# Probabilities times values as one fp32 product per head pair in a fused cross-attention and mixture-of-experts kernel

## The reference, cut to what matters

```python
# x: 8 batches x 512 queries x 512;  ctx: 8 x 64 keys x 128;  16 heads of 32
q  = layernorm(x) @ Wq.T                    # 512 x 512
k, v = split(ctx @ Wkv_expand.T)            # each 64 x 512 per batch
scores = (q_h @ k_h.T) / sqrt(32)           # per head h, 512 x 64
scores = where(causal, scores, min)         # query i sees keys 0..i
attn = softmax(scores)
o  = attn @ v_h                             # the product that is changed
x  = x + concat(o) @ Wout.T
h  = layernorm(x)
logits = h @ router_w.T                     # 8 experts, the two largest count
x  = x + sum over the 2 experts of logit * (silu(h @ wg) * (h @ wu)) @ wd
       + (silu(h @ sg_w + sg_b) * (h @ su_w + su_b)) @ sd_w + sd_b
```

## Time and profile before

| | |
|---|---|
| runs | 942.33 us median of 3 (939.0 to 943.42) |
| the profiled execution | 941.48 us, its span 939.8 us |
| TensorE busy | 818.6 us, 87% of the span |
| VectorE busy | 668.8 us, 71% |
| ScalarE busy | 446.3 us, 47% |
| GpSimd busy | 431.9 us, 46% |
| chain that ended last | 62% TensorE, 16% VectorE, 8% issue, 6% GpSimd, 6% ScalarE |

### The profile page before, as it was taken

The page is one execution under the profiler, slowest core; times in us unless marked ns, Lnnn a source line. Parts: engine busy times, 40 slices in busy tenths (PEclk is TensorE's granted clock), DMA queues, the critical chain, the costliest instruction groups (busy, mean ns, idle before and its releaser), DMA issues.

```text
span 939.8 us, 19907 instructions
## 1 busy us (share of the span) xinstructions
PE 818.6 (87%) x6538; PEld 520.9 (55%) x6538; DVE 668.8 (71%) x1206; ACT 446.3 (47%) x817; POOL 431.9 (46%) x509
## 2 busy tenths in 40 slices
PE   5659999998999989999898721499999999999995
PEld 2546766666676766667675311255555555555552
DVE  4889898988989989899897349655445555445552
ACT  3545667676766767676674410132223232223221
POOL 1013454544545445455453434345555555555553
PEclk9789999999999999999999755599999999999998
DMA  8203123141131411412111000246666667666671
GB/s 313 90 12 111 58 55 125 69 121 57 46 131 47 141 56 45 131 45 66 44 55 43 35 23 1 57 87 119 112 106 117 121 108 119 114 115 114 113 116 16
DMA packets 36464, 81.09 MB, mean 86 GB/s; under 512 B 8448, under 2 KB 9472, under 8 KB 35008
## 3 DMA queue, kind: packets, MB, share of 16 engines
q0 software_dynamic: 15904, 35.70, 21.7%
q1 hardware_dynamic: 20512, 44.73, 14.5%
HBM read 46.71 MB, written 35.53 MB: 88 GB/s over the span
## 4 chain that ended last, share of the span: by engine, by line
PE 62%; DVE 16%; issue 8%; POOL 6%; ACT 6%; DMA 1%; ACTq 0%; DVEq 0%; POOLq 0%
PE psum L1098 38%; PE psum L1089 11%; PE psum L1159 7%; DVE hid L912 4%; PE psum L1195 3%; PE psum L1173 2%; ACT kv_store L561 2%; ACT xn1T L561 1%; DVE xn1T L728 1%; POOL xy L466 1%; POOL exp_all L450 1%; DVE stats L799 1%; DVE xy L843 1%; POOL probsT L520 1%; POOL gate_up L470 1%
## 5 line engine op out<-in xcount | busy, mean ns | idle before, releaser
L1074 DVE SCALAR_TENSOR_TENSOR hid<-psum,gate_up,attn 128x256 f32<-128x256 f32 x71 | 34.4, 484 | 158.1 <-ACT attn L686 158.1
L543 POOL DMA_INDIRECT out<-w_q,gate_up x71 | 112.5, 1584 | 43.6 <-issue 17.4
L533 POOL DMA_INDIRECT x_in<-normed_tokens,gate_up x71 | 70.6, 994 | 116.0 <-DVE y_w L1071 112.4
L686 ACT ACTIVATE attn<-psum,gate_up 128x256 f32<-128x256 f32 x71 | 33.7, 474 | 165.1 <-PE psum L1098 165.1
L1159 PE MATMUL psum<-xn1T,w_q 128*128 128x128 f16 x1536 | 93.5, 222 | 12.7 <-DVE xy L843 9.8
L1098 PE MATMUL psum<-exp_all,hidT 128*128 x426 | 103.5, 379 | 1.0 <-DVE hidT L1061 1.0
L1098 PE MATMUL psum<-exp_all,xn2T 128*128 x432 | 101.7, 386 | 2.9 <-DVE xn2T L728 2.9
L1159 PEld LDWEIGHTS psum<-xn1T,w_q 128*128 128x128 f16 x1536 | 90.4, 100 | 15.4 <-issue 15.1
L1098 PE MATMUL psum<-exp_all,attnT 128*128 x420 | 96.4, 379 | 0.0
L1098 PE MATMUL psum<-w_sh,xn2T 128*128 128x512 f16 x384 | 89.5, 383 | 3.4 <-DVE xn2T L728 3.4
L1098 PE MATMUL psum<-w_o,attnT 128*128 128x512 f16 x384 | 88.1, 379 | 1.6 <-DVE attnT L894 1.6
(11 more groups left out here) (191 smaller groups left out, 1763.8 us busy)
## 6 DMA issues: line engine op xcount, KB each, us to landing
exp_all<-experts SPq DMA_DIRECT2D x8, 1536.0 KB, 8.1
normed_tokens<-xn SPq DMA_DIRECT2D x32, 260.0 KB, 2.6
x_in<-x SPq DMA_DIRECT2D x32, 256.0 KB, 2.8
out<-xy SPq DMA_DIRECT2D x32, 256.0 KB, 2.0
exp_all<-shared SPq DMA_DIRECT2D x1, 1536.0 KB, 11.2
mag_rows<-magnitudes SPq DMA_DIRECT2D x8, 192.0 KB, 3.8
x_in<-normed_tokens,gate_up POOLq DMA_INDIRECT x71, 3.4
out<-w_q,gate_up POOLq DMA_INDIRECT x71, 4.8
```

Source lines behind the costliest of these rows:

```text
L533: pool.indirect_dma_start(x_in[:, t % 4, :], None, xn_dram, bass.IndirectOffsetOnAxis(gather_at[:, t:t + 1], 0)).then_inc(gathered[t % 4], 16)
L543: pool.indirect_dma_start(out, bass.IndirectOffsetOnAxis(add_at[:, t:t + 1], 0), y[:, t % Y_RING, :], None, bounds_check=TOKENS - 1, oob_i ...
L686: act.activation(silu_g, psum[:, GU_BANK, 0:I], ACT.Silu, scale=gate_scale_at[:, bass.ds(t - 2, 1)]).then_inc(silu_ready, 1)
L1074: dve.scalar_tensor_tensor(hid[:, :], psum[:, GU_BANK, I:2 * I], up_scale_at[:, bass.ds(t - 2, 1)], silu_g, ALU.mult, ALU.mult).then_inc(e ...
```

## The change

The transposed probabilities are kept as one fp32 tile, which ScalarE copies with scale 1 (before, 2^14); the two VectorE passes per tile are gone. The values are kept as fp32 too (ScalarE writes them with the same scale as before), their four VectorE passes are gone, and `v_bd` is fp32. Each head pair's product is one fp32 matmul in the program in place of three fp16 ones. The semaphores `probsT_hi`, `v_hi` and `v_split` go; `probsT_ready` and `v_ready` are now raised by ScalarE.

```diff
-        v_all = v_all.rearrange("p (v b r d) -> p v b r d", v=2, b=B, r=PAIRS)
+        v_all = v_all.rearrange("p (b r d) -> p b r d", b=B, r=PAIRS)
-        v_bd = v_bd.rearrange("p (v r h w) -> p v r h w", v=2, r=PAIRS, h=2)
+        v_bd = v_bd.rearrange("p (r h w) -> p r h w", r=PAIRS, h=2)
...
-        probsT = sb("probsT", [P, 2, PAIRS, P], F16)
+        probsT = sb("probsT", [P, PAIRS, P])
...
                     for h in range(2):
-                        copy(*value_parts(0, b, h), sc[SK * h:SK * h + SK, S_V:S_V + 1], v_hi)
+                        copy(*value_parts(b, h), sc[SK * h:SK * h + SK, S_V:S_V + 1], v_ready)
...
                     act.wait_ge(probsT_mm, t2 + 1)
                     for n in range(2):
-                        copy(probsT[:, 0, 4 * n:4 * n + 4, :], bank(n), P_UP, probsT_hi)
+                        copy(probsT[:, 4 * n:4 * n + 4, :].rearrange("p r q -> p (r q)"), bank(n), 1.0, probsT_ready)
...
-                        copy(v_bd[rows, :, :, h, 0:HD],
-                             v_all[rows, :, bass.ds(b, 1), :, :].rearrange("p v o r d -> p v (o r) d"), 1.0, v_bd_ready)
+                        copy(v_bd[rows, :, h, 0:HD],
+                             v_all[rows, bass.ds(b, 1), :, :].rearrange("p o r d -> p (o r) d"), 1.0, v_bd_ready)
...
-                for n, b in enumerate((0, 4)):
-                    for h in range(2):
-                        dve.wait_ge(v_hi, 2 * n + h + 1)
-                        dst, src = value_parts(1, b, h)
-                        low(dst, src, sc[SK * h:SK * h + SK, S_V:S_V + 1], value_parts(0, b, h)[0], v_split)
-                    if n == 0:
-                        dve.wait_ge(wq_hi, 1)
-                        low(w_q[:, 1, :], wq_raw, col(sc, S_TMP), w_q[:, 0, :], wq_split)
+                dve.wait_ge(wq_hi, 1)
+                low(w_q[:, 1, :], wq_raw, col(sc, S_TMP), w_q[:, 0, :], wq_split)
...
-                if live(t2):
-                    for n in range(2):
-                        dve.wait_ge(probsT_hi, 2 * t2 + n + 1)
-                        low(probsT[:, 1, 4 * n:4 * n + 4, :].rearrange("p r q -> p (r q)"), bank(n), P_UP,
-                            probsT[:, 0, 4 * n:4 * n + 4, :].rearrange("p r q -> p (r q)"), probsT_ready)
...
                     for r in range(PAIRS):
-                        dst = psum[:, r // 4, (r % 4) * 2 * VW:(r % 4 + 1) * 2 * VW]
-                        for a, z in PASSES:
-                            last = pe.matmul(dst, probsT[:, a, r, :], v_bd[:, z, r, :, :].rearrange("p h w -> p (h w)"),
-                                             start=(a == z == 0), stop=(a == 1))
+                        last = pe.matmul(psum[:, r // 4, (r % 4) * 2 * VW:(r % 4 + 1) * 2 * VW], probsT[:, r, :],
+                                         v_bd[:, r, :, :].rearrange("p h w -> p (h w)"), start=True, stop=True)
                     last.then_inc(av_mm, 1)
```

More of the change, by code:

```diff
@@ L113, in xattn_moe @@
         kv_store = sb("kv_store", [P, sum(sizes)])[:, :]
-        k_all, v_all, k_bd, v_bd = [kv_store[:, sum(sizes[:n]):sum(sizes[:n + 1])].bitcast(F16) for n in range(4)]
+        k_all, v_all, k_bd, v_bd = [kv_store[:, sum(sizes[:n]):sum(sizes[:n + 1])] for n in range(4)]
+        k_all, k_bd = k_all.bitcast(F16), k_bd.bitcast(F16)
         k_all = k_all.rearrange("p (v c k) -> p v c k", v=2, c=C)
-        v_all = v_all.rearrange("p (v b r d) -> p v b r d", v=2, b=B, r=PAIRS)
+        v_all = v_all.rearrange("p (b r d) -> p b r d", b=B, r=PAIRS)
         k_bd = k_bd.rearrange("p (v c h k) -> p v c h k", v=2, c=C, h=HPC)
-        v_bd = v_bd.rearrange("p (v r h w) -> p v r h w", v=2, r=PAIRS, h=2)
+        v_bd = v_bd.rearrange("p (r h w) -> p r h w", r=PAIRS, h=2)
         bd_flat = kv_store[:, sum(sizes[:2]):]
@@ L183, in xattn_moe @@
         hot_at, hot_hi = [a[:, 0:16 * SLOTS].rearrange("p (n k i s) -> p n k i s", n=2, k=2, i=4) for a in (
-            kv_store[:, 13 * TE:13 * TE + 8 * SLOTS].bitcast(F16), probsT[:, :, :, :].rearrange("p v r q -> p (v r q)"))]
+            kv_store[:, 13 * TE:13 * TE + 8 * SLOTS].bitcast(F16), probsT[:, :, :].rearrange("p r q -> p (r q)").bitcast(F16))]
         rest = kv_store[:, 13 * TE + 8 * SLOTS:]
@@ L226, in xattn_moe @@
             "wq_hi", "wq_split", "wo_hi", "wo_split", "wsh_hi", "wsh_split")]
-        k_mm, k_hi, k_split, v_mm, v_hi, v_split, k_bd_ready, v_bd_ready = [sem(n) for n in (
-            "k_mm", "k_hi", "k_split", "v_mm", "v_hi", "v_split", "k_bd_ready", "v_bd_ready")]
+        k_mm, k_hi, k_split, v_mm, v_ready, k_bd_ready, v_bd_ready = [sem(n) for n in (
+            "k_mm", "k_hi", "k_split", "v_mm", "v_ready", "k_bd_ready", "v_bd_ready")]
         expert_in, e_mags, e_mags_stored, e_mags_back, e_chain, e_scales_ready, piece_hi, piece_split = [
@@ L243, in xattn_moe @@
             "scores_mm", "masked", "max_ready", "shifted", "probs_ready")]
-        probsT_mm, probsT_hi, probsT_ready, av_mm, recip_ready, attn_ready = [sem(n) for n in (
-            "probsT_mm", "probsT_hi", "probsT_ready", "av_mm", "recip_ready", "attn_ready")]
+        probsT_mm, probsT_ready, av_mm, recip_ready, attn_ready = [sem(n) for n in (
+            "probsT_mm", "probsT_ready", "av_mm", "recip_ready", "attn_ready")]
         attnT_mm, attnT_hi, attnT_ready, proj_mm, x1_ready, x1b_ready = [sem(n) for n in (
@@ L324, in split_piece, with value_parts @@
             return w_exp[:, bass.ds(e, 1), v, k * PIECE:(k + 1) * PIECE].rearrange("p o w -> p (o w)")
-        def value_parts(v, b, h):
+        def value_parts(b, h):
             rows = slice(SK * h, SK * h + SK)
             at = (4 + b) % 8
-            return v_all[rows, v, b:b + 4, :, :], psum[rows, at:at + 4, :].rearrange(
+            return v_all[rows, b:b + 4, :, :], psum[rows, at:at + 4, :].rearrange(
                 "p b (r h d) -> p b r h d", h=2, d=HD)[:, :, :, h, :]
@@ L370, in step @@
                     sp.wait_ge(k_split, 1)
-                    sp.wait_ge(v_split, 4)
+                    sp.wait_ge(v_ready, 4)
                 if j == 0 and e is not None:
@@ L429, in _ @@
             for h in range(2):
-                pool.memset(v_bd[SK * h:SK * h + SK, 0, :, h, HD:VW], 1.0).then_inc(kv_zeroed, 1)
+                pool.memset(v_bd[SK * h:SK * h + SK, :, h, HD:VW], 1.0).then_inc(kv_zeroed, 1)
             pool.wait_ge(kv_zeroed, 3)
@@ L636, in step @@
                     if isinstance(b, int) and b == 0:
-                        act.wait_ge(v_split, 4)
+                        act.wait_ge(v_ready, 4)
                     for h in range(2):
@@ L1137, in first_products @@
                     values(b)
-                pe.wait_ge(v_split, 2)
+                pe.wait_ge(v_ready, 2)
             pe.wait_ge(const_ready, 3)
@@ L1187, in step @@
                     if isinstance(t1, int) and t1 == 0:
-                        pe.wait_ge(v_split, 4)
+                        pe.wait_ge(v_ready, 4)
                     wait(pe, shifted, t1)
```

## The result

The kernel after the change takes 968.15 us, median of 4 runs (967.41 to 971.19), against 941.88 us (939.0 to 943.42, 4 runs) before: a ratio of 1.0289, interval 1.0255 to 1.0322. It is slower, by 26 us from median to median.

What follows compares the result with a forecast made beforehand. TensorE was taken as the bound in the attention stage. +27.8 us from the longer product, -3.3 at the start and -1.5 at the end gave +23.0 on 941.48, forecast as 965 us, between 960 and 970, wider range 950 to 977.

Steps and rivals of the forecast that it cites:

- The product: Probabilities times values on TensorE: 16 fp32 records paced by their loads, 1.74 us per tile, 1.0 us more than before.
- How many tiles pay: Attention tiles 2 to 30: 22 pay 1.0 us each, 7 mask steps 0.8 us each, together +27.8 us.
- The two waits: TensorE's waits per batch, 1.10 us for x1 and 1.30 us for hid, would stay and not absorb the growth.
- VectorE's passes are worth nothing in the middle: Two passes per tile over transposed probabilities, 1.2 us a pair, lie beside TensorE's work; removing them in 29 tiles gains nothing.
- The start: First tiles, set by VectorE: 2.1 us saved up to qT and 1.19 us at tile 0's probabilities, -3.3 us.
- The end: Tile 31's product starts 2.2 us earlier without VectorE's low parts; at most some 1.5 us gained.
- ScalarE's copy: Copy of the transposed probabilities, now fp32: between 594 and 684 ns, at most 0.2 us more per tile, taken as 0.
- The stream alone: Rival 1, fp32 product: loads hidden, +0.18 us in each of 29 tiles, +0.4 in all, 942 us; chance 0.06.
- load and stream in turn: Rival 2, fp32 product: load and stream follow each other, +1.9 us per full-paying tile, +49, 990 us; chance 0.07.
- the estimate of 941 us: Skill page's count of four fp32 passes alone: 0.88 us for the product per tile, no change; loads not counted.
- VectorE giving back: Rival 3, attention stage: the two waits per batch absorb growth in 15 tiles, 14 pay, +9, 951 us; chance 0.07.
- The cheap fp32 product: Rival 4: one cycle per column, 30 ns per record, product 0.49 us per tile, -12, 929 us; chance 0.04.

Runs made afterwards that it cites:

- the ladder: Changed kernel with unread fp32 products of several weight and streamed widths, then 24 fp16 products, appended at TensorE's end; 975.2 us in one run.
- the half weights: Changed kernel with each fp32 product taking only the first 64 queries as weights, other 64 queries' values left out; 951.4 us, ratio 1.0104 to the kernel before.
- the kernel without low parts: Kernel before, without VectorE's low-part passes over probabilities and values, its 24 fp16 matmuls per tile kept on high parts; 935.36 us, ratio 0.9943.
- another order: Changed kernel with expert scales one step later and, in mask steps, gate_up ahead of the shift and hid ahead of xn1T; 957.33 us, ratio 1.0159 to the kernel before.

## Why the prediction was right

Its time of 965 us was 3 us under the median, the span's growth 25.9 us against a predicted 23.0. The mechanism held; the terms were off by up to 2.7 us each and in part cancelled.

- **The product.** Predicted 1.74 us, measured 1.79; the growth per tile 1.0 and measured 1.05 us. The mechanism, that the longer of load and stream sets the pace, is shown by the ladder (no change from 8 to 33 streamed columns, half the period with half the weight columns) and in its place by the half weights. The matmul's record was forecast at 221 ns and is 275: the fp16 record of 193 ns has 166 over its stream of 66 columns (27.5 ns at 2.4 GHz), and I had added the fp32 stream of 55 ns to these 166; what is added is the longer of stream and load (166 + 109). With half the weights it is 222 ns (166 + 56).
- **How many tiles pay.** Predicted 22 of the 29 in full and 0.8 us in the 7 mask steps. With these terms the recorded 27.8 is 22.0 + 5.6 = 27.6 us, a slip of 0.2. The mask steps grew by 0.97 us (15.47 to 16.44), so nearly no slack took it up: that makes 1.2 us in all. The middle is 29.20 us and tile 30's 1.06, 30.3 us where 27.6 should have stood; without the 7 mask steps that leaves (30.3 - 7 x 0.97) / 22 = 1.07 for each of the others, against 1.0: 1.5 us more.
- **The two waits.** That they would not take up the growth is right: 1.09 and 1.28 us, against 1.10 and 1.30. Both chains start behind the product.
- **VectorE's passes are worth nothing in the middle.** Shown from both sides: taken away alone they gave nothing in 28 steps (416.78 against 416.71 us), and put back they cost nothing there (445.98 against 445.91). VectorE's busy time fell by 40.1 us where 49 were forecast as a sum of single passes; a pair back to back takes 1.19 us and not twice 0.685, which makes 5.8 of the difference in 32 tiles.
- **The start.** Predicted -3.3, measured -1.73 us. The first L1149 starts at 26.18 us as forecast, qT is copied at 31.25 (before 33.37, -2.1), tile 0's product no longer waits for VectorE. Then the scores of tile 0 took 2.74 us where they had taken 1.48:

```profile
32.63 2.74 PE L1183 MATMUL psum<-kv_store,qT 128*128 128x256 f16 x12 [3.61 <-DVE qT L729]
```

  TensorE had stood still 3.61 us before them, and they ran at half the clock. Twelve profiles have the same scores after the same 3.6 us. In seven they took 2.74 us, and there the first query projection had started at 25.92 us or later (here 26.18); in four they took 1.48, and in one 1.74 us, and there it had started at 25.80 or earlier. The ladder's profile is the plainest case, since its program is the same up to its end: projection at 25.42, scores in 1.48, and 77.36 us where this one has 79.50 and the kernel before 81.23. That is a start of -3.9 us against the predicted 3.3. So the term was about right, and 2.1 us of it were lost to an earlier delay of 0.76 and to the clock. Why the scores run at full clock in the executions that start them earlier stays open.
- **The end.** Predicted -1.5, measured -1.1 us before routing: tile 31's product waits 1.18 us for ScalarE (forecast 1.3) instead of 3.36 for VectorE, and is 1.1 us longer itself. The further 1.5 us after routing, from a clock that was back earlier, were not in the sum. Without them the growth would have been 27.4 us, and 4.4 us over the sum instead of 2.9: that part of the closeness is luck.
- **ScalarE's copy** costs 595 against 594 ns: nothing, as taken; the upper bound of 684 was far.

**The rivals.** The stream alone (942 us) and load and stream in turn (990 us) fall to the ladder. The Trainium skill (FP8 and Floating Point Precision, TensorE Precision Notes) counts four passes for fp32, which agrees with the ladder's streams: 0.109 us for 128 columns and record. That section says nothing of the load. The load, 0.11 us per record here, is nearly the whole difference between the estimate of 941 us and what was measured: 1.79 us of L1161 against the 0.88 of that estimate make 26.4 us in 29 tiles. VectorE giving back (951 us) falls to the unchanged middle of the kernel without low parts and to the two waits, which kept their length, though another order gets 12 us after the change. The cheap fp32 product (929 us) falls to the first row of the chain.

## What to carry to other kernels

Before three fp16 products are folded into one fp32 product, compare its load with its stream: with 128 weight columns and 66 streamed its two records cost 0.22 us against 0.09 for three fp16 matmuls. With 128 streamed it would be 0.22 against 3 x 0.056 = 0.17 us, an estimate from the ladder's 0.11 us per load and 0.109 per stream, since that size ran at half clock there. So the fold has to earn its cost on another engine. Take an engine's relief as worth nothing until something waits for the end of its queue. Here it was worth nothing in the given order, and only after the change did another order give 12 us.

## What was not expected of the hardware

- An fp32 weight load costs by its columns: 0.11 us for 128 and no more than 0.058 for 64, twice per product, at full clock. An fp16 load of 128 columns keeps pace with 0.031 us.
- The recorded duration of a matmul in a row of like ones was mostly 166 ns and, to within some 6 ns, the pace: 275 for the fp32 records of the change (pace 0.112 us), 222 with half the weight columns (0.058 in the ladder, 0.062 in the kernel), 273 with 64 weight columns and 128 streamed (0.109). So the median duration hints at the pace before any timeline is read. It is no rule: with 8 streamed columns the ladder's records are 256 ns long at a pace of 0.11 us.
- After the same idle time of 3.6 us the same matmuls ran at half clock in seven profiles (2.74 us) and at full clock in four (1.48 us), and of the kernel after and the ladder, which are one program up to there, one is on each side.
